# A kernel of four layers on one core: the last layer's routing in groups of nine tiles, its dense sums in three staggered lanes

## What is computed

```python
def _L1_conv_ref(x, Wq, Wk, Wv, gamma):        # attention, per image, N = 576 positions
    q, k, v = x @ Wq, x @ Wk, x @ Wv
    energy = jnp.einsum('bid,bjd->bij', k, q)
    attn = jax.nn.softmax(energy, axis=-1)
    return gamma * jnp.einsum('bij,bjc->bic', attn, v)

def _L1_ffn_ref(x, switch_w, switch_b, expert_w, expert_b):   # 4608 positions, 16 experts
    probs = jax.nn.softmax(xf @ switch_w.T + switch_b, axis=-1)
    route_probs, routes = jnp.max(probs, axis=-1), jnp.argmax(probs, axis=-1)
    pos = (number of earlier positions with the same route)
    keep = pos < capacity                       # int(1.2 * 4608 / 16) = 345
    buf[routes, pos] = xf                       # kept positions only
    y = jnp.einsum('ecd,efd->ecf', buf, expert_w) + expert_b[:, None, :]
    return jnp.where(keep[:, None], y[routes, pos], xf) * route_probs[:, None]
```

## Time and profile before

| | before |
|---|---|
| three runs, us | 453.04, 451.37, 449.98 |
| median, us | 451.37 |
| profiled execution, us | 448.98 |
| its span, us | 446.8 |
| its mean granted TensorE clock | 0.865 |
| busy: PE, DVE, ACT, POOL | 373.4 (84%), 305.2 (68%), 154.1 (34%), 127.8 (29%) |
| chain that ended last: PE, POOL, DVE, ACT | 24%, 8%, 6%, 4% of the span |

### The profile page before, as it was taken

One profiled execution on the slowest core, in us unless ns is written; L12 is line 12 of the kernel. 1 busy time (PEld: TensorE's weight loads), 2 busy tenths in 40 slices (PEclk: granted clock), 3 DMA queues, 4 the chain that ended last, 5 costly groups with the idle time before them and its releaser, 6 DMA issues. The chain is left out here.

```text
span 446.8 us, 6657 instructions
## 1 busy us (share of the span) xinstructions
PE 373.4 (84%) x2125; PEld 315.9 (71%) x2125; DVE 305.2 (68%) x949; ACT 154.1 (34%) x324; POOL 127.8 (29%) x141
## 2 busy tenths in 40 slices
PE   5955949968999999998756999999789796699880
PEld 5955949947888887887445899999779762693330
DVE  5846884885555566569656576876574969259997
ACT  2221154434333333332214455475465530240000
POOL 5750143006500000002000366010116567005773
PEclk9999555558999999999856599999999976699996
DMA  8930510005700000000011011111001011772335
GB/s 182 278 119 12 164 43 1 1 0 203 292 1 0 0 1 0 0 0 0 2 28 43 10 35 35 34 35 35 1 1 55 13 41 48 256 264 82 95 99 147
DMA packets 22890, 29.66 MB, mean 66 GB/s; under 512 B 4104, under 2 KB 18249, under 8 KB 22606
## 3 DMA queue, kind: packets, MB, share of 16 engines
q1 hardware_dynamic: 18350, 22.47, 17.1%
q0 software_dynamic: 1728, 3.54, 2.6%
q10 hardware_dynamic: 2784, 3.29, 2.1%
HBM read 13.48 MB, written 12.78 MB: 59 GB/s over the span
## 5 line engine op out<-in xcount | busy, mean ns | idle before, releaser
L158 POOL TENSOR_TENSOR rstd<-sm,neg_half 128x9 f32<-128x9 f32 x10 | 18.0, 1804 | 203.3 <-DVE sm L152 203.3
L807 PE MATMUL ps<-wide,gu_w 128*128 (+1 forms) x108 | 51.9, 481 | 2.2 <-PEq L704 2.2
L879 ACT ACTIVATE s<-ps 128x384 f32<-128x384 f32 (+1 forms) x60 | 29.5, 492 | 67.4 <-PE ps L811 67.0
L1767 PE MATMUL ps<-V,wide 128*128 128x129 f32 x400 | 51.3, 276 | 0.0
L838 PE MATMUL ps<-h,wd 128*128 128x384 f32 x120 | 49.8, 497 | 1.6 <-DVE h L923 1.2
L1767 PEld LDWEIGHTS ps<-V,wide 128*128 128x128 f32 x400 | 48.4, 192 | 0.1
L918 DVE TENSOR_TENSOR t<-ps,s 128x384 f32<-128x384 f32 x48 | 26.8, 557 | 30.3 <-ACT s L879 30.0
L1811 PE MATMUL ps<-ew,xTd 128*128 128x512 f32 x72 | 38.2, 669 | 3.6 <-DVE R L1480 3.5
L1480 DVE SCALAR_TENSOR_TENSOR R<-ps,dense_w,R 128x128 f32<-128x128 f32 x144 | 38.3, 343 | 1.3 <-PE ps L1811 1.1
L1232 DVE TENSOR_REDUCE mx<-ps 128x1 f32<-128x576 f32 (+1 forms) x40 | 29.8, 749 | 12.8 <-PE ps L1735 12.7
L811 PE MATMUL ps<-wide,gu_w 128*128 (+1 forms) x108 | 37.0, 343 | 0.3 <-DVE t L918 0.3
(11 more groups left out here) (252 smaller groups left out, 810.8 us busy)
## 6 DMA issues: line engine op xcount, KB each, us to landing
slots<-zrow SPq DMA_DIRECT2D x7, 768.0 KB, 7.7
xe<-slots SPq DMA_DIRECT2D x16, 192.0 KB, 4.0
slots<-wide ACTq DMA_DIRECT2D x16, 192.0 KB, 2.9
xall<-in_x SPq DMA_DIRECT2D x8, 288.0 KB, 6.1
out<-R SPq DMA_DIRECT2D x9, 192.0 KB, 2.1
Q<-sQK SPq DMA_DIRECT2D x8, 144.0 KB, 2.4
K<-sQK SPq DMA_DIRECT2D x8, 144.0 KB, 2.5
ew<-in_ew SPq DMA_DIRECT2D x1, 1024.0 KB, 5.4
```

The source lines that it names most:

```text
L807: nc.tensor.matmul(o, gu_w[0][:, w], xTH[:, at], start=True, stop=False)
L879: nc.scalar.activation(s4[q][:r], bank[q][:r, :CH], ACT.Silu).then_inc(s_ok[q], 1)
L1767: last = nc.tensor.matmul(bank[6 + k // 3][:, k % 3 * (C + 1):(k % 3 + 1) * (C + 1)], PT[n % 2][:, jk, i0:i0 + P], V[n % 2][:, jk, :], sta ...
```

## The change

It replaces the ragged groups by four of nine tiles. Groups 0 and 1 are routed whole within steps 5 and 6, each with nine transpositions (four, four and one, the last of them in a free corner of the bank of the transposed energies), nine logits and one bias addition; group 2 is normalised on VectorE in step 7, and its logits stand between the last image's attend blocks; group 3, the dense tiles, follows. The dense tiles are summed in three lanes of three tiles, a lane four sums behind the one before it; each product of one tile by four experts (a unit) has one of four banks. Seven units and 20 sums stand ahead of the experts, three units and 20 sums in the expert loop, 26 units and 113 sums behind it.

```diff
-        GROUP = ((0, 9), (9, 18), (18, 31), (31, 36))
-        TAIL = ((18, 21), (21, 24), (24, 27), (27, 31), (31, 34), (34, 36))
-        SETS = ((27, 28), (29, 30), (31, 32), (33, 34, 35))
+        LANES, UNIT_BANK = 3, (0, 1, 6, 7)
+        SUMS = [(lane_tile(lane, k // (E1 + 1)), (k % (E1 + 1) or None) and k % (E1 + 1) - 1)
+                for _, lane, k in sorted((3 * k + 4 * lane, lane, k) for lane in range(LANES)
+                                         for k in range(GT // LANES * (E1 + 1)))]
+        SUMS_AHEAD, UNITS_AHEAD, UNIT_AT = 20, 7, (5, 9, 12)
+        SUMS_EACH = [1 + (e % 4 == 3) for e in range(E1)]
+        COMBINE_AT = [24 + 12 * j for j in range(ROUTED * 3 - 1)]
+        PART = ((0, 4), (4, 8), (8, GT))
+        ROUTED_IN = {B - 3: 0, B - 2: 1}
# GpSimd
-                rstd_tail(2)
-                scatter(1, range(0, SPLIT))
-                rstd_tail(3)
-                scatter(1, range(SPLIT, GT))
+                rstd6(2)
+                scatter(1, range(GT))
+                rstd6(3)
                 scatter(2, range(GT))
# VectorE, in the step loop
+                        if k == 2 and g is not None:
+                            add_bias(g)
+                        if k == 3 and 0 <= n - 1 < B and n < B - 1:
                             attended(n - 1, (0, 1, 2))
+                        if k == 3 and g is not None:
+                            route_max(g)
+                            route_first(g)
+                        if k == 4 and g is not None:
+                            route_slot(g)
+                    if n == B - 1:
+                        dve.wait_ge(o_ok, NB_SS * (B - 2))
+                        for t in range(GT):
+                            ins = nc.vector.bn_stats(st[0][:, t, :], R[:, GT * 2 + t, :])
+                        norm_moments(d, ins, GT, 0, P, EPS_T, var6, mean=-0.5)
+                        place_counts(1)
+                        place_sums(1)
+                        place_index(1)
+                        attended(B - 2, (0, 1, 2))
+                        dve.wait_ge(rs6, 5)
+                        dve.wait_ge(sc6[0], 16 * GT)
+                        for t in range(GT):
+                            ins = nc.vector.tensor_scalar(xn[0][:, t, :], R[:, GT * 2 + t, :], ...)
# VectorE, with the experts
-                experts7(0, E1)
+                sums(0, SUMS_AHEAD)
+                for e in range(E1):
+                    expert7(e)
+                    sums(count, count + SUMS_EACH[e])
# ScalarE, in the step loop
+                        if n == B - 3 and k == 4:
+                            act.wait_ge(rs6, 4)
+                            normalise(1, 0)
+                        if n == B - 2 and k == 0:
+                            normalise(1, 1)
+                            normalise(1, 2)
# TensorE, in the step loop and behind it
+                        if k == 1 and g is not None:
+                            banks_empty()
+                            router_transposes(g, 0)
+                            router_transposes(g, 1)
                         if 0 <= n < B:
+                            energies_T(n, k, g)
                         if k == 2 and g is not None:
+                            logits(g)
+                        if k == 4 and n == B - 1:
+                            banks_empty()
+                            for c in range(3):
+                                router_transposes(2, c)
+                    if g is not None:
+                        counts(g)
+                attend(B - 1, 0)
+                logits(2)
+                for k in range(1, NB_SS):
                     attend(B - 1, k)
+                counts(2)
+                banks_empty()
+                for c in range(3):
+                    router_transposes(3, c)
+                logits(3)
+                counts(3)
+                for u in range(UNITS_AHEAD):
+                    dense(u)
# TensorE, in the expert loop
+                    if e in UNIT_AT:
+                        dense(unit)
+                        unit += 1
```

More of the change, by code:

```diff
@@ L1460, in _ @@
                 route_slot(2)
-                place_counts(2, bank[5])
+                place_counts(2)
                 place_sums(2)
                 place_index(2)
-                weigh_dense(2)
+                add_bias(3)
+                route_max(3)
+                route_first(3)
+                place_counts(3)
+                place_sums(3)
+                weigh_dense()
                 def combine(part):
@@ L1933, in expert_bias @@
-                def expert_bias(first, end, b, done=True):
-                    for t in range(first, end):
-                        last = nc.tensor.matmul(bank[b][:, (t - first) * P:(t - first + 1) * P],
-                                                wT[:, (t - DENSE0) * P:(t - DENSE0 + 1) * P], ebr[:], start=True, stop=True)
-                    if done:
-                        last.then_inc(b9, 1)
-                for j in range(4, 9):
-                    dense(j)
-                pe.wait_ge(ye7, E1)
@@ L1959, in metaformer_kernel @@
+                pe.wait_ge(wc9, 1)
+                for i, b in enumerate(BIAS_AT):
+                    for j in range(3):
+                        t = 3 * i + j
+                        last = nc.tensor.matmul(bank[b][:, j * P:(j + 1) * P], wT[:, t * P:(t + 1) * P], ebr[:],
+                                                start=True, stop=True)
+                    last.then_inc(b9, 1)
+                for u in range(unit, NUNIT):
+                    dense(u)
         local.close()
```

589 lines of the change are left out of this document (207 added, 382 removed).

## The result

The changed kernel takes 453.57 us (median of 18 runs), the kernel before beside it 450.4: ratio 1.0057, interval [1.0035, 1.008]. By the ratio the change costs about 2.6 us (1.6 to 3.6 by the interval), where the prediction had 1.0 us gained. The profiled execution has a span of 450.9.

What follows compares the result with a forecast made beforehand. A serial end bounds it: third group's indices, expert loop, 41.5 us tail. Last result 0.7 earlier plus tail 0.3 shorter gives -1.0: 450.4 us median from 451.37, no change that can be told (0.65); range 446.2 to 455.6.

Steps and rivals of the forecast that it cites:

- Step 4: Image step before the rerouted ones, 292.26 to 304.57: nothing moves up to its end.
- Steps 5 and 6: Image steps routing all of groups 0 and 1: 17.2 and 16.5 us, with TensorE waits of 1.1 and 1.3.
- the faster rival: Waits put into steps 5, 6 and 7 don't come; up to 4.7 us earlier, 445.7; chance 0.23.
- Step 7: Last image's step: TensorE waits 2.3 and 0.6 for xn; last attend block ends at 356.9, today 353.4.
- Group 2's indices: From the last attend block 8.6 us to the last scatters, at 365.5, 2.8 earlier than today.
- Ahead of the experts: Seven dense products cost nothing, as rows come at 382.4; the fifth transposition starts at 385.2, 3.3 earlier.
- The third rival: Group 3's weights, not the rows, start the experts; fifth transposition at 388.3, time 453.5; chance 0.17.
- The loop: Expert loop: three dense products add 2.65 us, twenty sums cost nothing; last result at 402.2.
- The slower rival: Sums between the expert additions are on the path, 20 x 0.26 = 5.2 us, time 455.6; chance 0.2.
- The tail: Last result to last add: 41.2 us, with GpSimd's gather chain at 41.5 or less and VectorE at 40.2.
- the Trainium skill's rule: VectorE instructions with two SBUF inputs contend with GpSimd reading SBUF; gathers would lose 1.4, leaving VectorE's tail of 40.2.
- The sum: Last result 0.7 earlier and tail 0.3 shorter: 1.0 us gained in all.

Runs made afterwards that it cites:

- the kernels of the table: The changed kernel and follow-up variants of it, each measured beside the kernel before; ratios from 0.9921 to 1.0082.
- both stretches filled: Changed kernel with identity transpositions into an idle bank, 16 in step 7's wait and 76 from the last attend block to group 3's counts; 448.95 us, ratio 0.9938.
- attend first: Changed kernel with image 6's last attend block and image 7's first moved ahead of group 2's transpositions on TensorE in step 7; ratio 0.9951.
- places later: Changed kernel with group 1's sums and row indices moved behind group 2's normalisation on VectorE in step 7; ratio 1.0038.
- group 3 filled: Changed kernel with 76 identity transpositions into an idle bank in TensorE's waits from the last attend block to group 3's counts; ratio 0.998.
- no products in the loop: Changed kernel with no dense products in the expert loop, 8 sums there for 20 and 125 in the tail for 113; ratio 1.0082.
- step 7 filled: Changed kernel with sixteen identity transpositions into an idle bank where TensorE waits for xn in step 7; ratio 0.9994.
- attend first with group 3 filled: Changed kernel with two attend blocks ahead of group 2's transpositions and 76 identity transpositions in the waits up to group 3's counts; ratio 0.9938.
- its run of six split: Kernel before with the second gathered part added mid-way through the next step's dense sums; longest gather 1.56 us for 2.35, no ratio given.

## Why the prediction was wrong, point by point

Two steps of the prediction failed: it priced the work behind TensorE's waits at full clock, and it put the change of step 4 at nothing.

*Step 4: put at nothing.* The prediction has "up to 304.57 nothing moves". But group 0 is normalised in step 4, and its larger pieces on ScalarE make the step 0.56 longer (12.87 for 12.31).

*Steps 5 and 6: right.* Step 6 starts at 321.90 (321.8 predicted), step 7 at 338.60 (338.3), both after the subtraction. The waits that the faster rival wanted away came in steps 5 to 7: 0.97, 1.37 and 2.02, for 1.1, 1.3 and 2.3.

*Step 7: the wait right, its price wrong.* The prediction had `xn` at 346.5 and a wait of 2.3 + 0.6; TensorE went on at 347.09 after a wait of 2.02. But the sentence "Two blocks (four last 4.79, 1.05 each between others) from 348.15, the nine logits, 1.9, four blocks, 4.8: the last ends at 356.9" prices everything behind the wait at full clock. It ended at 360.0: 3.1 more. Of that, 0.6 is `xn` coming later, and 2.5 goes when the wait is filled. The earlier trace rows had shown what a sparse stretch does to the clock, and the prediction used it for group 3 alone, not for a wait that it had itself put into a stretch without one.

*Group 2's indices: the step right, its start wrong.* From the last block 8.6 was predicted and 9.0 passed (the counts at half clock). With 3.1 on its start, the gain of 2.8 became a loss of 0.7. The prediction had named last scatters behind 368 as a sign of being wrong, and this sign came.

*Ahead of the experts: wrong.* "I count nothing, since the rows come at 382.4" failed with the weights: ready "between 374 and 376.5" by the prediction, 380.1 in the trace (the end of `drop_w` at 381.65, less 1.57), because the attend blocks were late and the logits took 4.02. TensorE was free at 386.1, not between 379.5 and 383.0; it is 3.1 beyond the bound for half clock, and 3.1 is what step 7 had lost. The third rival named this gate, with the fifth transposition at 388.3 and 453.5 us; it is 389.3 and 453.57. The gate is right, but that the times agree so well is luck: the rival had the half clock of group 3 and not that of step 7, and it shows no working for 388.3. From its own 383.0 the fifth transposition would follow at about 386.2, since 3.24 pass from the first to the fifth here. It also had the lesser chance.

*The loop: right.* The three turns are 1.86 for 1.0, 2.58 in sum for 2.65; the twenty sums cost nothing, VectorE still idles 0.18 in most turns with one sum. The slower rival (sums on the path) didn't come. What the prediction did not say is that the products are paid back in the tail, shown by the run without them.

*The tail: 40.56 for 41.2.* The prediction took GpSimd's chain as the bound; in the trace it is VectorE, and the gathers span 32.5 for 34.4. By the Trainium skill's rule ("SBUF — State Buffer", "Who interferes with whom") the prediction had 40.2. The trace does not show that rule at work: gathers and runs of adds with both operands in SBUF do overlap (a gather from 420.50 to 421.44, a run from 420.65 to 421.52), and neither is longer for it. That 40.56 lies between the two figures proves neither, since the kernels of the table with the same 113 sums in the tail have 40.05 to 41.62 there.

*The sum.* 4.1 at the fifth transposition (389.3 for 385.2), less 0.6 of the tail, is the 3.5 between +2.5 and -1.0; the 0.56 of step 4 comes on top. The run with both stretches filled is the kernel that the prediction described: after the start of step 7 it has the last block at 18.88 (18.6 predicted), the scatters at 27.54 (27.2), the fifth transposition at 46.85 (46.9), the last result at 63.81 (63.9). Its ratio is 2.8 us under the kernel before for the 1.0 forecast; a tail of 40.05 for 41.2 is 1.2 of that, and the rest lies within the interval. So from step 5 on the order of the work was read rightly, and the step that failed is one: durations taken at full clock behind waits of 2 and 5 us. That filling TensorE's waits alone brings these times back is shown; how much of the loss each of the two stretches owns is not a sum, since each gate hides the other (1.79 and 1.54 alone, 3.88 together).

## What to carry to other kernels

When a change makes TensorE wait in a stretch where it was busy, price the work behind the wait at both levels of the clock, and look for work already at hand (here two attend blocks) to put under it. Where a change cuts work into other pieces, look at every step in which a piece runs, also ahead of the stretch that it is about. Where two chains meet at one gate, gaining on one alone shows only up to the other. Before calling work in a loop a loss, ask which engine sets the stretch behind the loop and how much of its work that buys.

## What the runs showed of the hardware

- The granted clock behind a wait, one trace each: 0.50 after 2.02 us of waiting in the changed kernel, 1.00 after 0.86 in the four kernels with attend first and after 1.31 in the one with places later, 1.00 after the same wait filled with transpositions. The same wait did not always cost the same. In three kernels alike up to there (changed, group 3 filled, no products in the loop) it was 2.00 to 2.02 and the clock fell each time, but in the third only at 352, behind the nine transpositions; the last attend block ended 21.40, 21.30 and 20.52 after the start of step 7.
- A TensorE whose records fill its time does not always have the full clock. In four kernels (step 7 filled, group 3 filled, places later, attend first with group 3 filled) windows of the tail show a clock of 0.52 to 0.63 over 4 us with 2.00 of 2.00 us busy, behind the nine transpositions and the nine products with the expert biases; in the changed kernel, with the same instructions there, it was 1.00. In those four VectorE waits 1.5 to 1.9 in sum for dense products instead of 0.5. No run here tells when this drop comes.
- Seven gathers in these traces took 1.34 to 2.35. Each began 0.09 to 0.35 into a run of VectorE adds with both operands in SBUF and ended 0.81 to 0.83 after the run: 1.56 for a run that ended at 423.18, and in the kernel before 2.35, where the run was of six. None that began ahead of a run was stretched. But some that began as far inside one were not, either: 0.95 at 0.28 into a run in the kernel before with its run of six split, 0.95 at 0.32 in the one with places later. The Trainium skill's rule cited above says which pairs contend; these rows add that a gather that is held up waits out the whole run, and leave open which are.
- The last store of a result landed after 1.9 to 2.1 us or after 2.8 to 3.0, from kernel to kernel, and the first gather began later by as much. No run here tells why.
